# One-hots of node numbers on GpSimd instead of VectorE, and the merged rows' stores on ScalarE's queue, in the merge of a two-layer graph network

## The chip, the cores and the metric

One Trainium2 chip, one of its cores. The metric is the device time of one execution in microseconds; three runs of the kernel before are at hand. Engines are named as in the profile: PE is TensorE (PEld its weight loads), DVE is VectorE, ACT is ScalarE, POOL is GpSimd, SP is SyncE; a name with a q (SPq, ACTq, POOLq) is that engine's own instruction queue, where DMAs are issued.

## What is computed

The input is 50,000 nodes with 128 features, 50,000 edges sorted by target node, and 32 edge types. The change lies in the first layer, an attention layer with four heads:

```python
xl = (x @ Wl).reshape(n, H, C)
xr = (x @ Wr).reshape(n, H, C)
m = xl[src] + xr[dst]                       # edges, and a self loop for each node
e = leaky_relu(m, 0.2)
logits = einsum('ehc,hc->eh', e, att)
ex = exp(logits - amax[dst])
alpha = ex / (segment_sum(ex, dst) + 1e-16)
out = segment_sum(alpha * xl[src], dst)     # one row per node
# then a norm over all nodes (mean and variance of each feature), elu,
# layernorm of x + result, and a second graph layer with 2 rounds
```

## The kernel before, in words

The kernel is a sequence of stages; all five engines meet at the end of each (`end_stage`, `end_pool_stage`). Stage 0 projects all nodes (`xl_d`, `xr_d`), stage 1 works through the edges in 400 tiles and leaves in `w_d[0]` one row for each target node that has edges: 128 weighted sums, 4 denominators, 4 maxima, and the node's number in the last column (`WIDE` is 137). These rows are packed: the rows of a block of 128 nodes begin at a place that is looked up in `node_at`, and 128 rows from there hold all of that block.

Stage 2, the merge, is where the change lies. It puts the packed rows at their nodes, joins them with each node's self loop, and leaves `conv_d`. A tile is 128 nodes, a quad four tiles (98 quads, `QUADS`), a pair two quads (49 pairs, `PAIRS`), and a batch two pairs, so there are 24 full batches and one pair (`BATCHES` 25). For each pair:

- SP loads three of a quad's four tiles of packed rows (`load_sums`) and ACT's queue the fourth (`last_load`). The buffers hold six quads (`RING`), and a load for quad q waits until PE is done with quad q-6. SP also loads the nodes' own rows from `xl_d` (`load_own_rows`).
- DVE makes the one-hots (`pair_matrix`, lines 1872 to 1883): it subtracts the tile's first node number from the number column (L1877, once for each quad), and compares the result with 0 to 127 for all eight tiles in one instruction of 1024 columns (L1882). Two pairs of one-hots have room. It waits for the pair's packed rows and for PE to have used the one-hots of two pairs ago.
- PE multiplies one-hot by packed rows, one matmul for each tile (`gather_sums`, L1083), into two sets of PSUM banks by turns, and later adds up the merged rows and their squares over all nodes (`sums`, L1092).
- ACT copies PSUM into `agg_pair` and `dens` (`aggregated`, L1336 and L1337; it waits until the pair four back is merged), makes the exponentials of a batch (`share_exps`, L1343) and the squares of merged rows (`squares`, L1350).
- DVE computes the shares of edge sums and self loop for a batch (`share_args`, `share_values`, ten small instructions from L1891 to L1916), and merges a pair with three instructions of 1024 columns (`merged`, L1929, L1930, L1932), all of them on SBUF.
- POOL stores each merged quad to `conv_d` (L884), as soon as `cv_ok` says that its pair is merged. Semaphore `r["nh_out"]` counts the stores; `merged` waits for the stores of the pair three back, whose buffer it takes.

DVE's order is written out by hand: for batch v it is `pair_matrix(2v+2)`, `share_args(v)`, `share_values(v-1)`, `merged(2v-2)`, `pair_matrix(2v+3)`, `merged(2v-1)`. ACT's loop over pairs u is `aggregated` of both quads of pair u with a `last_load` behind each, then `squares` of the two quads of pair u-4, and every second time `share_exps`. `share_args(v)` needs `aggregated` of pair 2v+1, and that needs `merged(2v-3)`; so the two engines hand the work back and forth once in each batch. The stage ends with the norm's statistics on DVE and a square root on ACT (L1371), and stage 3 reads `conv_d` again.

Of the kernel before, what the change touches and what calls it, by code (L numbers as in the profile page):

```python
# [12 lines left out]
P = 128  # L13
# [39 lines left out]
def after(eng, sem, count):  # L53

    if not isinstance(count, int) or count > 0:
        eng.wait_ge(sem, count)
# [101 lines left out]
def gnn_kernel(nc, x, src, dst, etype, Wl, Wr, att, bias_conv, gn_weight, gn_bias, gn_mean_scale,  # L158
               basis, comp, loop_w, bias, out):
    ctx = ExitStack()  # L160
    with ctx:
# [240 lines left out]
        def pair_tiles(u):  # L402
            return quad_tiles(2 * u) + quad_tiles(2 * u + 1)
# [104 lines left out]
        def saved(l, q):  # L508

            return (q_in if q % RING // 3 else xl_out)[q % 3] if l else r["nh_out"][q % 3]  # L510

        def wait_saved(eng, l, q, stores):

            base = merged_counts["nh_out"][q % 3]
            eng.wait_ge(saved(l, q), (2 * base if l and q % RING < 3 else base) + 16 * stores)

        def wait_free(eng, l, q):

# [17 lines left out]
        def _(sp):  # L536
# [170 lines left out]
            sp.wait_ge(r["m_ps"], QUADS - 2)  # L707
            sp.wait_ge(cv_ok, PAIRS)
            for q in range(3):
                sp.wait_ge(r["nh_out"][q], 16)  # L710
                load_nx(q)
            end_stage(sp, 2)

# [58 lines left out]
        def _(pool):  # L772
# [104 lines left out]
            end_pool_stage(1)  # L877


            for q in range(QUADS):  # L880
                after(pool, r["nh_out"][q % 3], 16 * (q // 3))
                pool.wait_ge(cv_ok, q // 2 + 1)
                for to, part in node_quad(conv_d, q, of_pair(merged_pair, q), False):
                    pool.dma_start(to, part).then_inc(r["nh_out"][q % 3], 16)  # L884
            for k in range(3):
                pool.wait_ge(r["nh_out"][k], merged_counts["nh_out"][k])
            end_pool_stage(2)

            def inverse_row_deviation(q):
# [344 lines left out]
        def _(act):  # L1234
# [110 lines left out]
            def squares(q):  # L1345
# [3 lines left out]
                    act.wait_ge(cv_mm, q - 2)  # L1349
                act.activation(quad(4, q % 3)[:, 0:n, :], of_pair(merged_pair, q), ACT.Square).then_inc(cv_sq, 1)  # L1350

            def last_load(q):
                if q < QUADS:
                    if q >= RING:
                        act.wait_ge(r["m_ps"], q - RING + 1)
                    load_packed(act, -1, q, 3, 4)
            for q in range(4):
                last_load(q)
            for u in range(PAIRS + 4):
                if u < PAIRS:  # L1360
                    aggregated(2 * u)
                    last_load(2 * u + 4)
                    aggregated(2 * u + 1)
                    last_load(2 * u + 5)
                if u >= 4:
                    squares(2 * u - 8)
                    squares(2 * u - 7)
                if u % 2 and u < PAIRS or u == PAIRS - 1:
                    share_exps(u // 2)
            act.wait_ge(gn_var, 1)  # L1370
            act.activation(stat[:, 5, :], stat[:, 4, :], ACT.Sqrt).then_inc(gn_std, 1)  # L1371
            act.activation(join[:, 7, :], ones[0:1, 0:H], ACT.Exp)
# [151 lines left out]
        def _(dve):  # L1524
# [344 lines left out]

            dve.memset(work[12][:, 0:512], 0.0).then_inc(zeroed, 1)  # L1870

            def pair_matrix(u):
                n = pair_tiles(u)
                for q in (2 * u, 2 * u + 1):
                    at = slice(4 * q, 4 * q + quad_tiles(q))
                    wait_packed(dve, -1, q)
                    st.did(dve.tensor_tensor(node_rel[:, at], packed(q, WIDE)[:, 0:quad_tiles(q), WIDE - 1], node_base[:, at],  # L1877
                                             ALU.subtract))
                st.wait()
                if u >= 2:  # L1880
                    dve.wait_ge(r["m_ps"], 2 * u - 2)
                dve.tensor_tensor(sel_pair(u), lane[:, :].unsqueeze(1).to_broadcast([P, n, P]),  # L1882
                                  node_rel[:, 8 * u:8 * u + n].unsqueeze(2).to_broadcast([P, n, P]), ALU.is_equal).then_inc(pair_sel, 1)

            def share_args(v):

# [31 lines left out]
            def merged(u):  # L1918

                v, at = u // 2, slice(8 * (u % 2), 8 * (u % 2) + pair_tiles(u))  # L1920
                conv, xl = merged_pair(u), own_pair(u)
                edge, own = shares[:, v % 2, 0, at, :], shares[:, v % 2, 1, at, :]
                for q in (2 * u, 2 * u + 1):
                    wait_rows(dve, -1, q)
                    after(dve, r["nh_out"][q % 3], 16 * (q // 3 - 1))
                if u >= 3:
                    dve.wait_ge(cv_mm, 2 * u - 4)
                st.wait()
                st.did(dve.tensor_tensor(by_head(conv), by_head(agg_pair(u)), per_head(edge), ALU.mult))  # L1929
                st.did(dve.tensor_tensor(by_head(xl), by_head(xl), per_head(own), ALU.mult))  # L1930
                st.wait()
                dve.tensor_tensor(conv, conv, xl, ALU.add).then_inc(cv_ok, 1)  # L1932

            pair_matrix(0)
            pair_matrix(1)
            for v in range(BATCHES + 1):
                if 2 * v + 2 < PAIRS:
                    pair_matrix(2 * v + 2)
                if v < BATCHES:
                    share_args(v)  # L1940
                if v:
                    share_values(v - 1)
                    merged(2 * v - 2)
                if 2 * v + 3 < PAIRS:
                    pair_matrix(2 * v + 3)
                if v and 2 * v - 1 < PAIRS:
                    merged(2 * v - 1)

# [209 lines left out]
```

## Time and profile before

| | us |
|---|---|
| median of the three runs | 3206.0 |
| lowest, highest | 3199.38, 3206.53 |
| the profiled execution's own time | 3217.4 |
| its span from first to last instruction | 3215.5 |

| share of the span busy | PE | PEld | DVE | ACT | POOL |
|---|---|---|---|---|---|
| whole kernel | 89% | 64% | 79% | 51% | 53% |

```profile
## 2 busy tenths in 40 slices
PE   4898799999858888999799999699989999968897
PEld 4888688888735555888455555488845555536665
DVE  5999899999958897888677777544457777759998
ACT  2555223222224444999566666444446666645665
POOL 1110577777502222777777777322267777735554
PEclk9999899999979998999899999899999999989999
DMA  6999688888658886998333333399933333339997
```

Each slice is 80 us. The merge stands in slices 12 to 16 (from 904 us to 1262 us); in it the digits of PE and DVE are 8 and 9, DMA is at 8, ACT at 4 and POOL at 2. The profiled execution took 11 us more than the median; sums are made against its own time and then carried over to the median.

### The profile page before, as it was taken

How to read it: one execution, taken by the hardware profiler on the slowest of the kernel's cores; microseconds unless marked ns; L12 is line 12 of the kernel's file. 1: busy time of each engine (PE TensorE's matmuls, PEld its weight loads, DVE VectorE, ACT ScalarE, POOL GpSimd, SP SyncE). 2: the span in 40 equal slices, each digit the busy share in tenths (PEclk: the TensorE clock that was granted, in tenths of full speed). 3: DMA queues.
4: the chain of work that ended last, by engine and by line, in shares of the span. 5: the costliest groups of instructions: out<-in, count | busy, mean ns of one | idle time of the engine just before them, and what ended most of it. 6: DMA issues, size and time to landing. Idle time of an engine off the chain costs nothing.

```text
span 3215.5 us, 64715 instructions
## 1 busy us (share of the span) xinstructions
PE 2852.2 (89%) x16743; PEld 2059.8 (64%) x16743; DVE 2553.5 (79%) x7856; ACT 1654.8 (51%) x3920; POOL 1690.3 (53%) x2037
## 2 busy tenths in 40 slices
PE   4898799999858888999799999699989999968897
PEld 4888688888735555888455555488845555536665
DVE  5999899999958897888677777544457777759998
ACT  2555223222224444999566666444446666645665
POOL 1110577777502222777777777322267777735554
PEclk9999899999979998999899999899999999989999
DMA  6999688888658886998333333399933333339997
GB/s 170 263 278 274 160 186 184 186 182 184 155 150 237 244 243 202 293 293 273 97 104 104 104 103 104 91 298 304 298 105 104 104 103 104 104 84 328 331 341 259
DMA packets 744191, 621.24 MB, mean 193 GB/s; under 512 B 75517, under 2 KB 624622, under 8 KB 743822
## 3 DMA queue, kind: packets, MB, share of 16 engines
q1 hardware_dynamic: 546308, 361.80, 39.2%
q0 software_dynamic: 54208, 130.20, 15.0%
q10 hardware_dynamic: 143306, 125.07, 13.5%
q8 instruction: 140, 2.29, 0.3%
q14 instruction: 229, 1.88, 0.2%
HBM read 382.65 MB, written 234.13 MB: 192 GB/s over the span
## 4 chain that ended last, share of the span: by engine, by line
POOL 25%; DMA 21%; DVE 17%; issue 13%; PE 12%; ACT 8%; ACTq 2%; SPq 2%; DVEq 0%; POOLq 0%
POOL work L912 24%; DMA w_d<-work 15%; ACT work L1399 4%; PE bank L1202 3%; PE bank L1209 3%; DMA work<-w_d 3%; ACT work L1391 2%; DVE work L1784 2%; DVE work L1713 1%; DVE work L1715 1%; DVE self_logit L1717 1%; PE bank L1222 1%; DVE work L1929 1%; PE bank L1176 1%; DVE work L1930 1%
## 5 line engine op out<-in xcount | busy, mean ns | idle before, releaser
L2043 DVE SCALAR_TENSOR_TENSOR work<-bank,coef,work 128x128 f32<-128x128 f32 x2400 | 674.9, 344 | 242.3 <-ACT work L1433 239.0
L1155 PE MATMUL bank<-basis_s,work 128*128 128x512 f32 x1600 | 756.6, 596 | 1.8 <-ACT work L1426 1.8
L870 POOL DMA_INDIRECT work<-xl_d,slot_src x400 | 384.3, 961 | 204.1 <-issue 202.3
L912 POOL DMA_INDIRECT work<-x_d,slot_src x400 | 383.7, 959 | 126.3 <-issue 121.6
L912 POOL DMA_INDIRECT work<-h_d,slot_src x400 | 383.0, 957 | 123.8 <-issue 121.6
L1433 ACT ACTIVATE work<-bank,coef 128x128 f32<-128x128 f32 x800 | 294.0, 367 | 227.1 <-PE bank L1155 227.1
L1155 PEld LDWEIGHTS bank<-basis_s,work 128*128 128x128 f32 x1600 | 274.8, 192 | 197.2 <-issue 192.9
L1166 PEld LDWEIGHTS bank<-work 128*126 128x126 f32 x1600 | 207.6, 189 | 101.6 <-issue 100.9
L1209 PEld LDWEIGHTS bank<-work 128*128 128x128 f32 x1552 | 205.2, 193 | 97.1 <-issue 92.4
L884 POOL DMA_DIRECT2D conv_d<-work x99 | 73.8, 750 | 322.1 <-DVE work L1932 313.5
L1202 PE MATMUL bank<-work,loop_s 128*128 128x512 f32 x392 | 211.3, 621 | 33.9 <-ACT work L1473 33.1
L992 PE MATMUL bank<-work 96*128 96x125 f32 x1600 | 236.1, 276 | 0.0
L992 PEld LDWEIGHTS bank<-work 96*128 96x128 f32 x1600 | 217.4, 196 | 6.9 <-issue 0.2
L1146 PEld LDWEIGHTS bank<-ident,work 128*128 128x128 f32 x800 | 85.3, 142 | 206.4 <-DMA work<-x_d,slot_src 90.2
L1166 PE MATMUL bank<-work 128*126 128x128 f32 x1600 | 209.6, 274 | 5.5 <-ACT work L1439 3.2
L1473 ACT ACTIVATE work<-bank 128x512 f32<-128x512 f32 x196 | 114.8, 586 | 183.4 <-issue 133.5
L1209 PE MATMUL bank<-work 128*128 128x128 f32 x1552 | 206.3, 276 | 1.5 <-DMA work<-w_d 1.5
L1278 ACT ACTIVATE work<-bank 128x512 f32<-128x512 f32 x100 | 59.7, 597 | 256.7 <-issue 185.3
L929 POOL DMA_DIRECT2D h_d<-work x99 | 53.7, 543 | 247.0 <-DVE work L2077 243.1
L1092 PE MATMUL bank<-work,ones 128*128 128x512 f32 x392 | 179.2, 601 | 4.7 <-ACT work L1350 4.7
L1127 PE MATMUL bank<-work,ident 128*128 128x128 f32 (+1 forms) x782 | 162.3, 290 | 21.3 <-DVE work L1993 21.1
L2077 DVE COPY work<-bank 128x512 f32<-128x512 f32 x97 | 67.1, 692 | 135.7 <-PE bank L1222 135.7
(274 smaller groups left out, 6632.2 us busy)
## 6 DMA issues: line engine op xcount, KB each, us to landing
w_d<-work SPq DMA_DIRECT2D x800, 62.5 KB
work<-in_x_dram SPq DMA_DIRECT2D x194, 256.0 KB, 4.4
work<-x_d SPq DMA_DIRECT2D x194, 256.0 KB, 4.5
work<-xr_d ACTq DMA_DIRECT2D x388, 96.0 KB
w_d<-work SPq DMA_DIRECT2D x400, 66.9 KB
work<-w_d SPq DMA_DIRECT2D x398, 64.0 KB, 3.4
work<-w_d ACTq DMA_DIRECT2D x390, 64.0 KB, 3.4
xl_d<-work SPq DMA_DIRECT2D x97, 256.0 KB, 3.0
```

The source lines that it names most:

```text
L870: pool.indirect_dma_start(gathered(i)[:, c, :], None, xl_d, bass.IndirectOffsetOnAxis(ap=slot_src[:, a:a + 1], axis=0)).then_inc(e_in[i % ...
L912: pool.indirect_dma_start(quad(0, i % 3)[:, c, :], None, (x1_d, h1_d)[l], bass.IndirectOffsetOnAxis(ap=slot_src[:, a:a + 1], axis=0)).then ...
L992: last = pe.matmul(both[:, c * P + 1:c * P + 1 + TE], window(c, i)[:, h, :], turned_pick(h, i)[:, c, :], start=False, stop=h == 1, skip_gr ...
L1092: last = pe.matmul(psum[b][:, 0:whole * D], ones[:, :], rows[:, 0:whole, :].rearrange("p t d -> p (t d)"), start=False, stop=False, skip_g ...
L1127: pe.matmul(to[0:rows, at], ident[0:rows, 0:rows], skip_rows(q)[0:rows, t, :], start=True, stop=False)
L1155: pe.matmul(psum[YBANKS[k % 5]][:, :], quad(1, i % 2)[:, c, :], basis_s[:, l, :, :].rearrange("k b n -> k (b n)"), start=True, stop=True). ...
L1166: last = pe.matmul(psum[5 + c // per_bank][0:SLOTS, o:o + width], quad(4, i % 3, SLOTS)[:, c, :], quad(2, i % 3, width)[:, c, :], start=Tr ...
L1202: pe.matmul(to[:, 0:m], loop_s[:, l, :], work[7][:, (q % 2) * 512:(q % 2) * 512 + m], start=True, stop=False, skip_group_check=True)
L1209: last = pe.matmul(at, packed(q, D)[:, t, :], sel.rearrange("r (t p) -> r t p", t=4), start=False, stop=t == n - 1, skip_group_check=True)
L1399: last = act.activation(quad(8, k)[0:rows, t, :], psum[2 + q % 4][0:rows, t * D:(t + 1) * D], ACT.Identity, bias=norm[0:rows, k, 1, t:t + ...
L1433: act.activation(quad(2, i % 3, width)[:, c, 0:D], psum[YBANKS[k % 5]][:, 0:D], ACT.Copy, scale=coef[:, i, l, c, 0:1]).then_inc(r["first"], 1)
L2043: ins = dve.scalar_tensor_tensor(o, psum[YBANKS[k % 5]][:, b * D:(b + 1) * D], coef[:, i, l, c, b:b + 1], o, ALU.mult, ALU.add)
```

## The change

All one-hots of the stage are made by POOL instead of DVE: the same two subtractions for a pair, then one comparison for each tile (`tensor_scalar` with the tile's column as its scalar, 128 columns each) in place of one comparison of 1024 columns. POOL no longer stores merged rows. ACT stores a quad right after its squares, on its own DMA queue; the stores are counted on `xr_out`, which stage 0 has used and left at `merged_counts["nh_out"]`. ACT waits for all stores before the square root. The waits of DVE (`merged`) and of SP (first loads of stage 3) are moved to the new semaphore, and `wait_saved` of the later layers counts `nh_out` from zero.

```diff
@@ sync
             for q in range(3):
-                sp.wait_ge(r["nh_out"][q], 16)
+                sp.wait_ge(xr_out[q], merged_counts["nh_out"][q] + 16)
                 load_nx(q)
@@ gpsimd
-            for q in range(QUADS):
-                after(pool, r["nh_out"][q % 3], 16 * (q // 3))
-                pool.wait_ge(cv_ok, q // 2 + 1)
-                for to, part in node_quad(conv_d, q, of_pair(merged_pair, q), False):
-                    pool.dma_start(to, part).then_inc(r["nh_out"][q % 3], 16)
-            for k in range(3):
-                pool.wait_ge(r["nh_out"][k], merged_counts["nh_out"][k])
+            def pair_matrix(u):
+                n = pair_tiles(u)
+                for q in (2 * u, 2 * u + 1):
+                    at = slice(4 * q, 4 * q + quad_tiles(q))
+                    wait_packed(pool, -1, q)
+                    st.did(pool.tensor_tensor(node_rel[:, at], packed(q, WIDE)[:, 0:quad_tiles(q), WIDE - 1], node_base[:, at],
+                                             ALU.subtract))
+                st.wait()
+                if u >= 2:
+                    pool.wait_ge(r["m_ps"], 2 * u - 2)
+                for t in range(n):
+                    last = pool.tensor_scalar(sel_pair(u)[:, t, :], lane[:, :], node_rel[:, 8 * u + t:8 * u + t + 1], None, ALU.is_equal)
+                last.then_inc(pair_sel, 1)
+            for u in range(PAIRS):
+                pair_matrix(u)
             end_pool_stage(2)
@@ scalar
+            def save_merged(q):
+                act.wait_ge(xr_out[q % 3], merged_counts["nh_out"][q % 3] + 16 * (q // 3))
+                for to, part in node_quad(conv_d, q, of_pair(merged_pair, q), False):
+                    act.dma_start(to, part).then_inc(xr_out[q % 3], 16)
+
@@
                 if u >= 4:
                     squares(2 * u - 8)
+                    save_merged(2 * u - 8)
                     squares(2 * u - 7)
+                    save_merged(2 * u - 7)
                 if u % 2 and u < PAIRS or u == PAIRS - 1:
                     share_exps(u // 2)
+            for k in range(3):
+                act.wait_ge(xr_out[k], 2 * merged_counts["nh_out"][k])
             act.wait_ge(gn_var, 1)
@@ vector
                     wait_rows(dve, -1, q)
-                    after(dve, r["nh_out"][q % 3], 16 * (q // 3 - 1))
+                    if q >= 6:
+                        dve.wait_ge(xr_out[q % 3], merged_counts["nh_out"][q % 3] + 16 * (q // 3 - 1))
@@
-            pair_matrix(0)
-            pair_matrix(1)
             for v in range(BATCHES + 1):
-                if 2 * v + 2 < PAIRS:
-                    pair_matrix(2 * v + 2)
                 if v < BATCHES:
                     share_args(v)
                 if v:
                     share_values(v - 1)
                     merged(2 * v - 2)
-                if 2 * v + 3 < PAIRS:
-                    pair_matrix(2 * v + 3)
                 if v and 2 * v - 1 < PAIRS:
                     merged(2 * v - 1)
```

## Rows read from the trace of the kernel before

**Rows 1.** Stretch view: busy us and (instructions) of PE, PEld, DVE, ACT, POOL, clock, DMA, GB/s.

```profile
940.00:1222.00 282.00, 240.31 (x1002) 146.59 (x1000) 252.63 (x461) 119.89 (x435) 61.50 (x83) 0.96 0.84 241
```

**Rows 2.** Chain of work: start us, us, what; first and last steady L1929.

```profile
932.98 1.23 DVE work L1929
...
1230.55 1.23 DVE work L1929
```

**Rows 3.** Timeline of DVE, one batch: start us, us, instruction.

```profile
1161.97 0.20 DVE L1891 TENSOR_SCALAR merge_s<-dens 128x64 f32<-128x64 f32 x1
...
1164.59 1.23 DVE L1929 TENSOR_TENSOR work<-work,shares 128x1024 f32<-128x1024 f32 x1
1165.73 1.22 DVE L1930 TENSOR_TENSOR work<-work,shares 128x1024 f32<-128x1024 f32 x1
1166.99 1.22 DVE L1932 TENSOR_TENSOR work<-work 128x1024 f32<-128x1024 f32 x1
...
1168.39 1.22 DVE L1882 TENSOR_TENSOR work<-lane,node_rel 128x1024 f32<-128x1024 f32 x1
```

**Rows 4.** View of waits from 940 to 1222 us: in total, times, longest.

```profile
ACT work L1336 <- DVE work L1932: 136.8, 42, 4.9
...
DVE node_rel L1877 <- DMA work<-w_d: 17.0, 17, 2.7
```

**Rows 5.** Timeline of ACT, same batch.

```profile
1159.85 0.39 ACT L1336 ACTIVATE work<-bank 128x256 f32<-128x256 f32 x1 [1.80 <-DVE work L1932]
...
1168.31 0.38 ACT L1336 ACTIVATE work<-bank 128x256 f32<-128x256 f32 x1 [4.83 <-DVE work L1932]
...
1170.30 1.15 ACT L1350 ACTIVATE work<-work 128x512 f32<-128x512 f32 x2 [0.18 <-issue]
```

**Rows 6.** Line view: ACT's stores of 256 KB in stage 3 (min/median/max ns).

```profile
L1406 ACTq DMA_DIRECT2D x_d<-work x99: 326/326/452, 1276.8 to 1536.1; - x99
```

**Rows 7.** DMA queues from 940 to 1222 us: packets, MB, share of 16 engines.

```profile
q1 hardware_dynamic: 81133, 39.96, 53.6%
q0 software_dynamic: 6650, 21.76, 21.7%
```

**Rows 8.** DMA queues from 60 to 250 us, stage 0.

```profile
q1 hardware_dynamic: 101398, 50.35, 96.0%
```

**Rows 9.** Line views of POOL instructions: count, min/median/max ns, starts, shapes.

```profile
L834 POOL TENSOR_SCALAR work<-work,type_of x25: 1531/1535/1961, 35.0 to 263.2; 128x500 f32<-128x500 bf16 x25
...
L777 POOL TENSOR_SCALAR_AFFINE_SELECT ident<-ident x1: 287/287/287, 1.5 to 1.5; 128x128 f32<-128x128 f32 x1
...
L925 POOL TENSOR_TENSOR norm<-norm x98: 192/199/201, 2901.5 to 3205.6; 128x4 f32<-128x4 f32 x97, 128x3 f32<-128x3 f32 x1
```

**Rows 10.** Timeline of POOL and DVE in stage 0: both held up.

```profile
68.76 0.69 DVE L1784 TENSOR_TENSOR work<-work 128x512 f32<-128x512 f32 x1
...
68.98 1.87 POOL L834 TENSOR_SCALAR work<-work,type_of 128x500 f32<-128x500 bf16 x1 [30.94 <-PE bank L1036]
...
69.49 1.05 DVE L1713 SCALAR_TENSOR_TENSOR work<-work 128x512 f32<-128x512 f32 x1
```

**Rows 11.** The same at 168 us: neither held up.

```profile
168.31 1.53 POOL L834 TENSOR_SCALAR work<-work,type_of 128x500 f32<-128x500 bf16 x1 [7.05 <-PE bank L1036]
...
168.93 0.69 DVE L1784 TENSOR_TENSOR work<-work 128x512 f32<-128x512 f32 x1
```

**Rows 12.** Timeline of DVE and POOL in stage 3.

```profile
1326.93 0.69 DVE L1993 SCALAR_TENSOR_TENSOR work<-work 128x512 f32<-128x512 f32 x1
1327.11 0.60 POOL L894 TENSOR_SCALAR norm<-moments 128x4 f32<-128x4 f32 x1 [0.86 <-DVE norm_arg L2012]
```

**Rows 13.** Line view of L884, the stores of merged rows on POOL's queue.

```profile
DMA to landing us min/median/max: 2.8/4.2/6.6
```

**Rows 14.** Timeline at the stage's end: last squares, last variance step.

```profile
1251.60 1.04 ACT L1350 ACTIVATE work<-work 128x512 f32<-128x512 f32 x2 [3.21 <-DVE work L1932]
...
1259.44 0.29 DVE L1969 SCALAR_TENSOR_TENSOR stat<-stat 128x128 f32<-128x128 f32 x1
```

More of the change, by code:

```diff
@@ L514, in wait_saved @@
             base = merged_counts["nh_out"][q % 3]
-            eng.wait_ge(saved(l, q), (2 * base if l and q % RING < 3 else base) + 16 * stores)
+            eng.wait_ge(saved(l, q), (0 if not l else 2 * base if q % RING < 3 else base) + 16 * stores)
         def wait_free(eng, l, q):
@@ L1870, in _ @@
             dve.memset(work[12][:, 0:512], 0.0).then_inc(zeroed, 1)
[L1872 to L1883, printed above, removed]
             def share_args(v):
```

## The prediction

> **What bounds the kernel now.** I read the page first, to place the stage: the change touches only the merge, some 358 us of a span of 3215.5. Then the stretch view over the stage's steady part, 940 to 1222 us [rows 1]: DVE is busy 252.6 of 282 us (90%), PE 240.3 (85%), the DMA engines 84%, ACT 119.9 (43%), POOL 61.5 (22%). Three resources are near full. That is what a reader is to keep in mind: who takes load off the fullest meets the next two at once.
>
> The chain of waits gives the beat. L1929 of the first pair starts at 932.98 and that of pair 44 at 1230.55 [rows 2]; between them lie 22 batches, so 297.6 / 22 = **13.5 us for a batch**. The timeline of one batch [rows 3, 5] shows how it is made up. The shares start at 1161.97, `merged` at 1164.59, its last instruction ends at 1166.99 + 1.22 = 1168.21; so shares cost 2.62 us and `merged` 3.62. Then come one-hots (L1882 at 1168.39), the second `merged`, and one-hots again. ACT starts a pair's `aggregated` 0.1 us after `merged` ends (1168.31), is through it at 1170.30 (2.0 us, a load issue behind each quad included) and has made the squares at 1171.45. For the odd pair it starts at 1159.85, and DVE's shares follow at 1161.97, 2.1 us later. In the view of waits ACT stands 136.8 us for `merged` [rows 4]; DVE stands only 17.0 us, and for late packed rows. So DVE is the bound, and the beat is DVE's sum.
>
> **What is taken away.** DVE loses per batch two comparisons of 1.22 us and four subtractions, about 3.0 us with their gaps, and the wait for packed rows, 17.0 us over 21 batches, 0.8 a batch. What is next to be late? Without one-hots `merged` follows `merged`. From the end of the first one (call it M), DVE ends the second at M + 3.6. ACT meanwhile does `aggregated` 2.1 and squares 1.15, free at M + 3.3, so it starts the odd pair's `aggregated` at M + 3.7 and the shares start at M + 5.8. Add 2.6 and 3.6: the round closes after **12.0 us**. That is the new beat if nothing else is slower: 1.5 us less, 33 us over 22 batches. It is not to be had in full: PE's work for a batch is 240.3 / 282 x 13.5 = 11.5 us and the DMA engines' 0.84 x 13.5 = 11.3.
>
> **The stores.** On POOL's queue the stores moved 21.76 MB in 21.7% of 282 us, 2.8 us a MB, in packets of 3.3 KB; rows of 512 bytes on SP's queue take 96.0% of 190 us for 50.35 MB, 3.6 us a MB [rows 7, 8]. A batch stores 1.05 MB, so on ACT's queue the DMA engines need about 0.85 us more, 12.15 in all. With three resources between 11.5 and 12.15 in a round of 12.0 I take 12.6 as the best beat that can be had. The issue costs ACT little: 0.33 us each [rows 6], issued while the square before it (0.6 us) still runs; bounds are 0 and four times 0.33. ACT's new wait is for the store three quads back, issued over a pair earlier, so it has landed; behind that wait stand the next squares, `share_exps` and `aggregated`, and for them PE and DVE. Packed rows that ACT loads now queue behind two stores of 256 KB; they are needed a batch later. `merged` waits for stores of the pair three back, now issued by ACT two iterations before it is needed: covered. I put the stores at nothing while the beat is above 13.
>
> **What is added: POOL's work.** For a batch it is 16 comparisons of 128 columns and four subtractions. The nearest row is L834, the same instruction (`is_equal` against a column scalar), 500 columns in 1.53 us [rows 9]. Scaled with the columns alone it gives 0.39 us for 128; the row's own split, below, gives 0.13 + 1.40 x 128/500 = **0.49 us**. Ends: 0.29 us (L777, 128x128 in and out, another operation) and 0.56 (if the 0.2 us of L925 is a fixed part and the rest scales). I take 0.49, by the same operation; its input is bf16 where the new one is f32, which is why the lower end stays open. A subtraction is 0.2 us (L925), four with their semaphore waits 1.0. POOL's free time for a batch: 16 x 0.49 + 1.0 = 8.8 us, well under 13.5 by itself. It would be hidden if POOL and DVE did not meet.
>
> They do meet, and the trace shows it. L834 starts at 68.98 beside L1784, which has two inputs in SBUF and ends at 69.45 [rows 10]. L834 then takes 1.87 us instead of 1.53; its end lies 1.40 us behind L1784's end, and in the ten cases of this kind (of 25) the distance is 1.40 or 1.41. L894 (four columns) ends at 1327.71, 0.09 behind the end of L1993, and takes 0.60 us for what is otherwise 0.2 [rows 12]. So **POOL waits until a DVE instruction with two SBUF inputs has ended.** The other way round: L1713, started 0.04 us after L1784, takes 1.05 instead of 0.69, so DVE is held 0.36 us by L834 (five cases, 0.32 to 0.37). But L1784 that starts 0.62 us into L834 is not held at all [rows 11]. So POOL holds DVE for the first part only, until about 0.13 + 0.42 us of 1.53; 0.42 us is 500 columns, so for 128 I take **0.11 us**.
>
> All three instructions of `merged` have two SBUF inputs. Beside 1.22 us of such work POOL gets one comparison: it waits for the end, takes 0.11 us while the next DVE instruction is held, computes on, and its next one waits again. In two `merged` POOL thus makes six comparisons, and they take 6 x (1.22 + 0.11) = 8.0 us. The other ten, 4.9 us, and the 1.0 us of subtractions must lie where DVE doesn't hold it: beside the shares (small instructions, I add 0.4 us for blocks) and while DVE waits for ACT. Sum: 8.0 + 4.9 + 1.0 + 0.4 = **14.3 us for a batch, POOL being the bound.** Late one-hots stop PE, then ACT, then the shares, so the time that POOL lacks appears as idle time of DVE.
>
> The Trainium skill, "SBUF — State Buffer", section "SBUF: two separate sides", speaks against this change: a DVE instruction with two SBUF inputs and a GpSimd instruction that reads SBUF exclude each other, and whoever starts first has the shared port pair for its whole instruction. The trace agrees on POOL's waiting, but not on DVE's: it was held 0.36 us by an instruction that went on for 1.4 [rows 10].
>
> **Start and end of the stage.** The first pair's one-hots, which nothing hides, take DVE 1.22 us as all do; POOL needs 8 x 0.49 = 3.9, 2.7 more. The next three pairs come with their loads and should hide most of theirs. I add 4 us; bounds 1 and 4 x 2.7 = 11. At the end ACT waits for the last stores before the square root: last squares end at 1252.6, the variance is there at 1259.7 [rows 14], and a store takes 4.2 us to land, 6.6 at most [rows 13], so this costs 0; at most 1, should the square root's table load come behind the wait.
>
> **The sum.** (14.3 - 13.5) x 22 = +17, +4 for the start: +21 us. The profiled execution's 3217.4 would become 3238; against the median of 3206.0, 11 lower, **3227**.
>
> **The rivals.**
> 1. *The gain comes through.* If a comparison costs 0.3 us and its hold on DVE falls into gaps, the beat is 12.6: -0.9 x 22 = -20, +4 at the start, 3190. For: POOL's 0.29 us row; the holds are short. Against: with POOL in the middle of DVE's back-to-back work each hold is DVE's loss. Deciding point: beat below 13.1. Chance 0.22.
> 2. *Break-even.* A comparison costs under 0.38 us, so POOL keeps up, but its holds lie in DVE's round: 12.0 + 6 x 0.11 + some 0.4 beside the shares = 13.1. -0.4 x 22 + 4 = -5, 3201. Chance 0.20.
> 3. *The forecast*, POOL the bound at 14.3, 3227, its own range 3216 to 3238. Chance 0.35.
> 4. *POOL doesn't get between back-to-back instructions.* L1930 starts 0.09 us before L1929 ends [rows 3], with no wait between; if POOL gets in only behind L1930 and L1932, it makes four in two `merged` and twelve outside: 7.8 + 5.9 + 1.4 = 15.1, +35 + 4, 3245. Chance 0.15.
> 5. *Each holds the other for its whole instruction.* Then 7.3 us of `merged`, POOL's 8.8 and at most the shares' 2.6 stand one behind another: 18.7, +114 + 4, 3324. Against it: DVE was held for 0.36 us only, and once not at all [rows 10, 11]. Chance 0.08. It is the rule of the Trainium skill that is named above, taken in full.
>
> That the change doesn't do what it says I leave out: the one-hots and stores are the same, only their engines differ.
>
> **How the numbers follow.** The likeliest is 3227. Low end 3186 (rival 1 with a beat of 12.4: -24 + 4), high end 3263 (rival 4 at 0.56 us a comparison: 15.9, +53, with the start's 4). About 0.3% (10 us) is what a measurement can tell: faster 0.22, same 0.20, slower 0.58.
>
> **What would show it.** In the profile after: the distance of L1929 from batch to batch (14.3; 12.6; 13.1; 15.1; 18.7); POOL's comparison at its shortest (0.49) and its median, which should be well above it, with ends just behind ends of `merged`; durations of L1929 to L1932 at 1.33 instead of 1.22; PE's `gather_sums` waiting for POOL; `aggregated` waiting for PE, not for DVE. Rival 1 is right if PE and DMA are above 90% and POOL idles. I am wrong in the first step if a comparison of 128 f32 columns costs 0.3 us, and in the second if the DVE instructions are not longer than before. Stores are wrongly priced if ACT's idle time is ended by them.

## The result and the profile after

| | before | after |
|---|---|---|
| median of the runs, us | 3206.3 | 3288.9 |
| lowest, highest | 3199.38, 3208.07 | 3285.72, 3290.73 |
| the profiled execution's own time | 3217.4 | 3285.7 |
| its span | 3215.5 | 3283.9 |

The ratio is 1.0263 [1.0247, 1.0278]: slower by 82.6 us. The direction was forecast, the size was not: 3227 was the value, 3263 the upper end.

In the code after, POOL's subtraction is L885 and its comparison L891; `gather_sums` is L1091 (before L1083) and `sums` L1100, `aggregated` L1344 and L1345, `squares` L1358, the stores L1363 on ACT's queue, the first share instruction L1896, and `merged` L1935, L1936 and L1938 (before L1929, L1930, L1932). First the page: totals and slices of 82 us.

```profile
PE 2882.1 (88%) x16743; PEld 2092.6 (64%) x16743; DVE 2492.7 (76%) x7709; ACT 1656.3 (50%) x3920; POOL 1973.1 (60%) x2427
...
PE   4998799999667777899799999889989999978887
...
DVE  5999899999645556788677777734457777758998
...
POOL 1110677777388997477777777512257777744554
...
DMA  7999577777466776799533333379943333329997
```

The merge fills slices 12 to 16. POOL is at 7 to 9 there, where it was at 0 and then at 2. Behind slice 12, in which the stage began, PE was at 8, DVE at 7 to 9 and DMA mostly at 8; now PE is at 7, DVE at 5 and 6, and DMA at 6 and 7. The stretch view of the steady part gives the numbers (columns as in [rows 1]):

```profile
940.00:1280.00 340.00, 251.54 (x974) 166.68 (x975) 195.61 (x320) 118.69 (x424) 305.16 (x407) 0.90 0.70 191
```

POOL is busy 305 of 340 us (90%), DVE 58%, PE 74%, DMA 70%. Three resources were near their limit; now one is, and it is a new one. The view of waits from 940 to 1260 us says what stands behind what (in total, times, longest):

```profile
DVE merge_s L1896 <- ACT dens L1345: 127.6, 19, 7.5
ACT work L1344 <- PE bank L1091: 102.4, 38, 5.4
PEld bank L1091 <- POOL work L891: 101.3, 19, 6.6
...
POOL node_rel L885 <- DMA work<-w_d: 29.3, 19, 2.5
```

Read from the third line up: PE waits for POOL's one-hots, ACT for PE's sums, DVE for ACT's copies. DVE's wait of 6.7 us a batch is time that POOL lacks. The beat, from the timeline of DVE, L1935 of the first pair and of pair 44 (start us, us):

```profile
931.08 1.22 DVE L1935 TENSOR_TENSOR work<-work,shares 128x1024 f32<-128x1024 f32 x1
...
1302.16 1.23 DVE L1935 TENSOR_TENSOR work<-work,shares 128x1024 f32<-128x1024 f32 x1
```

371.1 / 22 = **16.87 us for a batch** instead of 13.53 [rows 2]: +73.5 us. That is the loss. From the stage's first subtraction to the first `merged` it is 31.3 us instead of 25.4 (+5.9), and from pair 44 to PE's first matmul of the norm 33.1 instead of 31.6 (+1.5). Stage 1 ended 7.8 us earlier in this execution (the first subtraction starts at 899.77 instead of 907.59), and the stages behind took 4.7 less, both with code that the change doesn't touch: 73.5 + 5.9 + 1.5 - 7.8 - 4.7 = 68.4, the difference of the two spans. The rest, up to 82.6, is that the profiled execution before was 11 us above its median and the one after 3 below.

What POOL does in a batch is in its timeline (instructions of one line in a row are put together, x8):

```profile
1100.50 0.20 POOL L885 TENSOR_TENSOR node_rel<-work,node_base 128x4 f32<-128x4 f32 x1 [1.30 <-DMA work<-w_d]
1100.80 9.96 POOL L891 TENSOR_SCALAR work<-lane,node_rel 128x128 f32<-128x128 f32 x8
...
1111.16 4.64 POOL L891 TENSOR_SCALAR work<-lane,node_rel 128x128 f32<-128x128 f32 x8
...
1117.26 0.20 POOL L885 TENSOR_TENSOR node_rel<-work,node_base 128x4 f32<-128x4 f32 x1 [1.27 <-DMA work<-w_d]
```

From 1100.80 to the next batch's comparisons at 1117.55 there are 16.75 us: eight comparisons beside the two `merged`, 9.96; subtractions, 0.4; eight comparisons clear of `merged`, 4.64; subtractions and a wait for packed rows, 1.75. The two sets of eight are the same work, and one takes more than twice as long. Taken one by one (timeline of POOL):

```profile
1100.80 0.72 POOL L891 TENSOR_SCALAR work<-lane,node_rel 128x128 f32<-128x128 f32 x1
1101.50 2.51 POOL L891 TENSOR_SCALAR work<-lane,node_rel 128x128 f32<-128x128 f32 x1
1103.99 2.41 POOL L891 TENSOR_SCALAR work<-lane,node_rel 128x128 f32<-128x128 f32 x1
1106.39 1.33 POOL L891 TENSOR_SCALAR work<-lane,node_rel 128x128 f32<-128x128 f32 x1
1107.70 1.33 POOL L891 TENSOR_SCALAR work<-lane,node_rel 128x128 f32<-128x128 f32 x1
```

And DVE at the same time:

```profile
1101.27 1.23 DVE L1935 TENSOR_TENSOR work<-work,shares 128x1024 f32<-128x1024 f32 x1
1102.41 1.22 DVE L1936 TENSOR_TENSOR work<-work,shares 128x1024 f32<-128x1024 f32 x1
1103.66 1.23 DVE L1938 TENSOR_TENSOR work<-work 128x1024 f32<-128x1024 f32 x1
1104.80 1.22 DVE L1935 TENSOR_TENSOR work<-work,shares 128x1024 f32<-128x1024 f32 x1
1105.94 1.31 DVE L1936 TENSOR_TENSOR work<-work,shares 128x1024 f32<-128x1024 f32 x1
1107.28 1.27 DVE L1938 TENSOR_TENSOR work<-work 128x1024 f32<-128x1024 f32 x1
```

The comparison that starts at 1101.50 ends at 1104.01, 0.38 us behind the end of L1936 (1103.63); it has let the end of L1935 (1102.50) pass, where L1936 had already started at 1102.41. The next one lets the end of the first L1938 pass, and gets in behind L1935 (1106.02). The two after it get in at 1107.25 and 1108.55. So in the 7.3 us of two `merged` POOL gets in at four of six ends. Over the whole stage it is the same: in 20 of the 22 batches two comparisons take over 2 us and two some 1.33, in the other two it is one and three.

### The profile page after: what moved, and what is told of

The parts are those of the page before. It is cut to its first block, busy times and chain, and to the rows that moved or that the text cites. A ratio compares the mean times of both kernels' runs of the same rounds, so it can differ in the third digit from the quotient of the medians.

```text
span 3283.9 us, 64963 instructions
## 1 busy us (share of the span) xinstructions
PE 2882.1 (88%) x16743; PEld 2092.6 (64%) x16743; DVE 2492.7 (76%) x7709; ACT 1656.3 (50%) x3920; POOL 1973.1 (60%) x2427
## 4 chain that ended last, share of the span: by engine, by line
POOL 44%; issue 16%; DVE 13%; PE 13%; ACT 7%; DMA 4%; ACTq 2%; SPq 1%; DVEq 0%; POOLq 0%
POOL work L920 23%; POOL work L870 11%; POOL work L891 10%; ACT work L1416 4%; PE bank L1210 3%; PE bank L1217 3%; DVE work L1801 2%; DVE work L1730 2%; DVE work L1732 2%; DVE self_logit L1734 2%; ACT work L1408 1%; PE bank L1230 1%; PE bank L1184 1%; DVE work L2095 1%; DMA w_d<-work 1%
## 5 line engine op out<-in xcount | busy, mean ns | idle before, releaser
L891 POOL TENSOR_SCALAR work<-lane,node_rel 128x128 f32<-128x128 f32 x391 | 338.7, 885 | 4.8
L1217 PEld LDWEIGHTS bank<-work 128*128 128x128 f32 x1552 | 207.0, 194 | 97.7 <-issue 93.0
L1091 PE MATMUL bank<-work 128*128 128x136 f32 x782 | 141.3, 352 | 115.0 <-POOL work L891 115.0
L1091 PEld LDWEIGHTS bank<-work 128*128 128x128 f32 x782 | 133.8, 254 | 145.7 <-POOL work L891 135.2
L1344 ACT ACTIVATE work<-bank 128x256 f32<-128x256 f32 x196 | 72.0, 388 | 257.6 <-PE bank L1091 145.2
```

Source lines behind the costliest of these rows:

```text
L891: last = pool.tensor_scalar(sel_pair(u)[:, t, :], lane[:, :], node_rel[:, 8 * u + t:8 * u + t + 1], None, ALU.is_equal)
L1091: last = pe.matmul(psum[2 + 2 * (q % 2) + t // 2][:, o:o + D + 2 * H], of_pair(sel_pair, q)[:, t, :], packed(q, WIDE)[:, t, 0:D + 2 * H], ...
L1217: last = pe.matmul(at, packed(q, D)[:, t, :], sel.rearrange("r (t p) -> r t p", t=4), start=False, stop=t == n - 1, skip_group_check=True)
```

## The experiments

The theory: POOL is the bound, since it waits for DVE's instructions with two SBUF inputs, and late packed rows come on top. Against it stand that the stores on ACT's queue do it; that the wait for packed rows only fills time which POOL has anyway; that comparisons are slow beside DVE for another reason than the kind of its operands; and that it is the fixed cost of so many small instructions. In the expectations A is the theory, and other letters are what an experiment sets against it. "Batch" is always the mean over the same 22; each ratio is to the kernel before on the same chip.

**1. The stores alone** (the kernel before with `save_merged` on ACT; DVE keeps the one-hots).

```diff
-            for q in range(QUADS):
-                after(pool, r["nh_out"][q % 3], 16 * (q // 3))
...
                     squares(2 * u - 8)
+                    save_merged(2 * u - 8)
                     squares(2 * u - 7)
+                    save_merged(2 * u - 7)
```

> One part of the change alone: DVE keeps the one-hots, only the stores move from POOL's queue to ACT's. Theory A (the whole loss is POOL's one-hots, with POOL waiting for VectorE's two-input instructions): the stores cost nothing, 3206 within 6 us, batches stay at 13.5 us. Rival B (part of the loss is the stores: packets of 512 bytes need more DMA time and ACT waits for their landing): 3216 to 3230, packed rows arrive later and DVE's wait for them grows from 17 us to 30 or more.

Measured: 3209.8 against 3215.0, ratio 0.9986 [0.9975, 0.9996]; batch 13.29. The stretch from 940 to 1222 us:

```profile
940.00:1222.00 282.00, 241.38 (x1020) 151.42 (x1020) 257.38 (x466) 122.93 (x448) 0.00 (x0) 0.96 0.90 245
```

The DMA engines go from 84% [rows 1] to 90%, 0.6 us a batch, and nobody waits for them longer: the wait for packed rows [rows 4] is not among the large ones any more. With the stores moved, DVE stands for packed rows 0.5 us in all where it was 17.0; why they come earlier with the DMA engines busier is open. So the stores by themselves cost nothing in the batch. They do have a part at the stage's end. ACT's table load for the square root stands behind the variance here too, where it lay behind the last squares before:

```profile
1254.32 1.28 ACT L1373 ACT_TABLE_LOAD   x1 [7.18 <-DVE stat L1972]
```

That is some 1.3 us. The rest of the loss needs the one-hots on POOL. The one-hots alone, with the stores left on POOL's queue, were not run, so what the two do only together is not told apart.

**2. The wait for packed rows** (the kernel after; ACT's queue loads its tile two quads earlier).

```diff
-            for q in range(4):
+            for q in range(RING):
                 last_load(q)
...
-                    last_load(2 * u + 4)
+                    last_load(2 * u + 6)
                     aggregated(2 * u + 1)
-                    last_load(2 * u + 5)
+                    last_load(2 * u + 7)
```

> The changed kernel, with ACT's fourth-tile loads issued one pair earlier (they are for pair u+3 in ACT's iteration u instead of u+2). In the changed kernel a batch takes 16.9 us, and in it POOL waits some 1.4 us for packed rows. Theory A says that POOL is the bound, so each us that it doesn't wait comes off the batch: 15.5 to 15.7 us, total 3256 to 3265. Rival C (POOL's wait is only a gap that a later wait would fill, for PE or ACT): less than 8 us gained, 3281 or more.

Measured: 3258.8 against 3215.0, ratio 1.0138 [1.0117, 1.0160]; batch 15.30. The stretch, and the line view of its subtraction:

```profile
940.00:1222.00 282.00, 216.24 (x883) 137.87 (x884) 180.24 (x291) 108.35 (x388) 278.36 (x370) 0.93 0.79 212
...
L885 POOL TENSOR_TENSOR node_rel<-work,node_base 128x4 f32<-128x4 f32 x74 | 13.1, 200 | 0.0
```

POOL is busy 278 of 282 us and waits for no packed rows. The wait was worth 1.6 us a batch, nearly half of the loss of 3.3, and it is of a new kind. In the kernel after, ACT issues the load for pair u+2 behind `aggregated` of pair u, that waits for `gather_sums`, and that for POOL's one-hots; so POOL waits for a load that its own lateness has made late. The transfer itself is not slower: such a load lands 2.3 us after its issue in the median, where it was 3.4 before the change. The eight comparisons beside `merged` still take 9.7 to 10.1 us.

The kernel after shows one more link in that chain, TensorE's clock (timelines of PE and of ACT's queue, and a stretch of that time):

```profile
1101.11 2.02 PE L1091 MATMUL bank<-work 128*128 128x136 f32 x16
...
1110.81 3.31 PE L1091 MATMUL bank<-work 128*128 128x136 f32 x16 [4.25 <-POOL work L891]
...
1114.61 0.40 ACTq L467 DMA_DIRECT2D work<-w_d  x1
...
1112.50:1114.20 1.70, 1.70 (x9) 1.70 (x8) 0.00 (x0) 0.70 (x5) 1.70 (x4) 0.50 0.17 41
```

The columns of the last line are those of [rows 1]; the last but two is the granted clock. Behind PE's wait for one-hots (4.25 us) it is at 0.50, and `gather_sums` takes 3.31 us for a pair, where ten microseconds before it took 2.02 at 1.00. ACT's copy and the load stand behind it, and POOL then waits 1.27 us for that load. Of POOL's 21 waits for packed rows between 930 and 1300 us, 20 come behind a `gather_sums` of 3.1 to 3.9 us. As an estimate from these rows, most of the 1.5 us a batch that POOL waits is the 1.0 to 1.9 us that the lower clock adds there; no run takes it away by itself.

**3. The port** (the kernel after; the shares go to PSUM, so that two of `merged`'s three instructions read one input from PSUM and only the last, L1941 here, has two in SBUF).

```diff
+            share_ps = psum[6][:, 0:256].rearrange("p (v k t h) -> p v k t h", v=2, k=2, t=16)
...
-                edge, own = shares[:, v % 2, 0, at, :], shares[:, v % 2, 1, at, :]
+                edge, own = share_ps[:, v % 2, 0, at, :], share_ps[:, v % 2, 1, at, :]
```

> The changed kernel, with the shares written to a free PSUM bank, so that L1935 and L1936 read one operand from SBUF and one from PSUM and only L1938 still has two SBUF inputs. DVE's work stays the same size. Theory A (POOL stands behind two-input instructions of DVE): the eight comparisons that take 9.9 us beside the merge shrink to 6 to 7.5, a batch to 13.3 to 14.5 us, total 3210 to 3237. Rival D (POOL is slow by itself and through its late packed rows, and its waiting for DVE matters little): batch 16 us or more, total 3270 or more.

Measured: 3217.4 against 3215.0, ratio 1.0011 [0.9999, 1.0023]; batch 13.28. Nothing of POOL's work is taken away, DVE's instructions are the same in number and size, and 3.6 us of 16.87 are gone. (With the 1.6 of experiment 2 this is more than the loss: the two overlap, since POOL is no longer the only bound here, and `gather_sums` mostly takes 2.13 us again.) POOL's timeline:

```profile
1095.92 4.69 POOL L891 TENSOR_SCALAR work<-lane,node_rel 128x128 f32<-128x128 f32 x8
...
1101.01 5.53 POOL L891 TENSOR_SCALAR work<-lane,node_rel 128x128 f32<-128x128 f32 x8
...
1102.74 1.48 POOL L891 TENSOR_SCALAR work<-lane,node_rel 128x128 f32<-128x128 f32 x1
```

DVE's:

```profile
1102.53 1.23 DVE L1941 TENSOR_TENSOR work<-work 128x1024 f32<-128x1024 f32 x1
1103.67 1.22 DVE L1938 TENSOR_TENSOR work<-work,bank 128x1024 f32<-128x1024 f32 x1
```

The eight comparisons beside `merged` take 5.4 to 6.4 us instead of 10. The only long one in this stretch starts 0.2 us into L1941 and ends 0.46 behind its end (1103.76), though the next `merged` has begun: an instruction with one input in PSUM (`bank`) doesn't shut POOL out.

**4. Only the early loads, in the kernel before.** The same edit as in 2.

> The kernel before, with ACT's fourth-tile loads one pair earlier, as in the run above. DVE waits there 17 us for packed rows between 940 and 1222 us. If the cause of that wait is the place of ACT's loads behind its copies, it goes and the total is 3206 - 15 = 3191; if it is the DMA engines' load (84% busy), nothing moves: 3203 to 3209.

Measured: 3208.5 against 3215.0, ratio 0.9978 [0.9966, 0.9990]; batch 13.16. DVE's wait for packed rows (0.8 us a batch [rows 4]) is gone, but it brings only 0.37 a batch, less than I expected; in exchange DVE waits 12.4 us of 282 for ACT's `dens`, where it was 2.0.

**5. Edits 2 and 3 together, in the kernel after.**

> The changed kernel with both cures at once: shares in PSUM (batch 13.3 us alone) and ACT's loads a pair earlier (15.3 us alone, from 16.9). With both, POOL's work in a batch is 2 x 4.64 us of comparisons, some 0.9 of subtractions and at most 2 us of waiting for L1938: 12.2 us, below what PE (11.5) and the DMA engines (12.2) allow by little. Theory A: batch 12.5 to 12.9 us, 8 to 15 us faster than the kernel before on the same chip (ratio 0.995 to 0.9975). Rival E (DMA load and the round trip between DVE and ACT hold it where the run with PSUM alone stands): 13.2 us, ratio 0.999 to 1.001.

Measured: 3196.5 against 3201.6, ratio 0.9979 [0.9967, 0.9990]; batch 12.96. A gain, but of 5 us, where I expected 8 to 15. Stretch and waits:

```profile
940.00:1222.00 282.00, 246.97 (x1038) 150.79 (x1036) 209.79 (x351) 126.28 (x457) 244.04 (x423) 0.97 0.89 245
...
POOL node_rel L885 <- DMA work<-w_d: 23.6, 16, 3.2
```

The median batch takes 12.7 us; two of 14.5 and 16.9 lift the mean. With DMA at 89%, PE at 88% and POOL at 87% that median is close to the prediction's best beat, 12.6.

**6. Half of the pairs on each engine** (the kernel after with early loads, shares in SBUF; DVE makes the even pairs' one-hots, POOL the odd pairs').

```diff
-                last.then_inc(pair_sel, 1)
-            for u in range(PAIRS):
+                last.then_inc(pool_sel, 1)
+            for u in range(1, PAIRS, 2):
                 pair_matrix(u)
...
-                pe.wait_ge(pair_sel, q // 2 + 1)
+                pe.wait_ge(pool_sel if q // 2 % 2 else pair_sel, q // 4 + 1)
```

> One-hots split: DVE makes those of the even pairs, in the gap in which it waits for ACT, and POOL those of the odd pairs; ACT's loads a pair earlier; shares stay in SBUF. POOL has 8 comparisons a batch, so it cannot be the bound, and the batch should fall to DVE's round of 12.0 us plus a few holds, that is to the 12.6 us that PE and the DMA engines allow: ratio to the kernel before 0.993 to 0.996. If POOL's comparisons, each standing behind the merge (9.9 us for eight) and then started late, still stop PE, the batch is 13.2 us or more and the ratio 0.998 or more.

Measured: 3222.3 against 3201.6, ratio 1.0054 [1.0036, 1.0073]; batch 14.23. A miss: I expected a gain. The median batch takes 13.0 us; seven of the 22 take 15.7 to 18.9 and make the loss. POOL has half the comparisons, but eight of them still take up to 11.0 us where they fall beside `merged`, 13 of the 21 sets 8.4 or more; one of them:

```profile
1094.42 9.80 POOL L892 TENSOR_SCALAR work<-lane,node_rel 128x128 f32<-128x128 f32 x8
```

POOL also waits for packed rows here, 88.5 us of 282. So halving its load doesn't help enough: one pair's one-hots start late and then take long once they meet `merged`, and PE waits for them (52.5 us of 282). Which of the two counts is seen in 7.

**7. The same with the shares in PSUM.** Edit 3 added to 6.

> The split of the run above, with the shares in PSUM too. If the port is what remains to be lost in that run, this one is faster by 0.2 to 0.4 us a batch (5 to 9 us in all); if PE and the DMA engines are the bound by then, the two are the same within 3 us.

Measured: 3197.1 against 3201.6, ratio 0.9985 [0.9971, 0.9998]; batch 13.14. From 6 to 7 it is 25 us, where I expected less than 10 from the port: with half the work on POOL the port still made the loss. POOL's wait for packed rows is even longer in 7, 140.9 us of 282, so that wait by itself is not what cost the time in 6.

**8. What a comparison costs by its size** (the kernel after, each comparison over 64 columns).

```diff
-                    last = pool.tensor_scalar(sel_pair(u)[:, t, :], lane[:, :], node_rel[:, 8 * u + t:8 * u + t + 1], None, ALU.is_equal)
+                    last = pool.tensor_scalar(sel_pair(u)[:, t, 0:64], lane[:, 0:64], node_rel[:, 8 * u + t:8 * u + t + 1], None, ALU.is_equal)
```

> The changed kernel, with each comparison made over the first 64 of its 128 columns only; the other half of the one-hots is left out, so the sums of those nodes are not made. It tells what a comparison consists of. If half of its 0.58 us is fixed (a line through 500 columns in 1.53 us and 128 in 0.58 gives 0.25 us fixed and 2.6 ns a column), it takes 0.42 us, and a pair clear of the merge 3.3 us instead of 4.64. Theory A: beside the merge the waits rule, not the width: eight comparisons there still take 7.5 to 9.5 us, a batch 14.5 to 15.7 us, total 3238 to 3262. Rival F (the width is what counts there too): both stretches halve, batch 13.5 us or less, total 3217 or less.

Measured: 3255.0 against 3201.6, ratio 1.0156 [1.0132, 1.0181]; batch 15.96. Line view (min/median/max ns) and two stretches of the timeline:

```profile
L891 POOL TENSOR_SCALAR work<-lane,node_rel x391: 430/440/2568, 900.4 to 1272.6; 128x64 f32<-128x64 f32 x196
...
1099.77 7.75 POOL L891 TENSOR_SCALAR work<-lane,node_rel 128x64 f32<-128x64 f32 x8
...
1107.93 3.31 POOL L891 TENSOR_SCALAR work<-lane,node_rel 128x64 f32<-128x64 f32 x8
```

In a row it is 3.31 / 8 = 0.41 us for 64 columns and 4.64 / 8 = 0.58 for 128, so about 0.25 us fixed and 2.6 ns for a column. Half the columns take 0.9 us off a batch, far from half of POOL's 15: the waits stay. Seven of the twenty sets of eight beside `merged` take 7.75 us like the one shown, the others 8.9 to 9.2, against 9.7 to 10.1 for nearly all at 128 columns. The comparisons that wait through two instructions take 2.34 to 2.54 us, at 128 columns 2.38 to 2.73. (The batch is a little above the 14.5 to 15.7 that I expected, because POOL now waits 2.8 us a batch for packed rows, 49.6 in 282, where it was 1.5.)

**9. A gap at every end** (the kernel after; DVE waits on a semaphore ahead of each of the three instructions, so that none starts before the one ahead has ended).

```diff
                 st.wait()
+                if u:
+                    dve.wait_ge(cv_ok, u)
                 st.did(dve.tensor_tensor(by_head(conv), by_head(agg_pair(u)), per_head(edge), ALU.mult))
+                st.wait()
                 st.did(dve.tensor_tensor(by_head(xl), by_head(xl), per_head(own), ALU.mult))
```

> The changed kernel, with a semaphore wait of DVE on its own instruction before each of the three instructions of a merge (before, only L1938 had one). DVE gets about 0.1 us more to do at four places of a batch. Theory A2 (POOL can step in where DVE's next two-input instruction has not been started yet, and mostly not between instructions that overlap): POOL gets in at each of the six ends, the eight comparisons beside the merge take 8.0 to 8.7 us instead of 9.9, a batch 15.6 to 16.3 us instead of 16.9, total 3262 to 3280, and the three instructions grow to 1.3 us each. Rival G (a waiting POOL gets in or not regardless of gaps): the stretch stays at 9.7 or more, and the total at 3286 or more.

Measured: 3277.9 against 3209.9, ratio 1.0220 [1.0200, 1.0240]; batch 16.22. POOL's comparisons, one by one:

```profile
1102.80 1.56 POOL L891 TENSOR_SCALAR work<-lane,node_rel 128x128 f32<-128x128 f32 x1
1104.34 1.33 POOL L891 TENSOR_SCALAR work<-lane,node_rel 128x128 f32<-128x128 f32 x1
```

In the batch shown all six that meet `merged` take 1.33 to 1.56 us. Of all comparisons between 940 and 1260 us none takes over 1.7 us, where in the kernel after 36 take over 2: with a gap at the end POOL gets in at each. Yet the eight take mostly 9.1 to 9.5 us (8.6 to 9.7 in all) instead of 9.96, because the gaps lengthen the two `merged` from 7.3 to 7.8 us; I had expected 8.0 to 8.7. So the two missed ends cost about 0.65 us a batch, and the rest of the port's price is there with every end used.

**10 to 12. In search of a faster one.** 10 is the kernel before with the stores on ACT and the early loads; 11 is number 5, and 12 is number 7, with SP loading the nodes' own rows two quads later, so that packed rows come first:

```diff
-            for q in range(QUADS + 8):
+            for q in range(QUADS + 10):
...
-                if q >= 8:
-                    load_own_rows(q - 8)
+                if q >= 10:
+                    load_own_rows(q - 10)
```

> The kernel before with stores on ACT's queue and ACT's loads a pair earlier, DVE keeping the one-hots. Each of the two alone gave a batch of 13.3 and 13.15 us. DVE's own work is 13.1 us, so together they give no more than 13.1: ratio 0.997 to 0.998, as the early loads alone. If the stores' change had a gain of its own (POOL's descriptors off the DMA engines), it would be 0.996 or less.

> The fastest kernel so far (all one-hots on POOL, shares in PSUM, early loads; batch 12.96 us in the mean, most 12.5, some 14.5 and 16.9), with SP's loads of own rows issued two quads later. SP stands up to 6 us before such a load until a merge has freed its buffer, and loads of packed rows queue behind. If that makes the long batches, they go and the mean falls to 12.5 to 12.6 us: ratio 0.994 to 0.996. If the long batches come from the DMA engines' load (89% busy), nothing moves: 0.997 to 0.999.

> The same change of SP's order in the kernel with split one-hots, shares in PSUM and early loads (batch 13.1 us in the mean, most 12.5, some 15 to 17.7). With the long batches gone 12.4 to 12.5 us, ratio 0.993 to 0.995; otherwise 0.998.

Measured, each against 3209.9: 3207.4, ratio 0.9988 [0.9977, 1.0000], batch 13.30; 3209.9, 0.9998 [0.9989, 1.0008], batch 13.15; 3207.9, 0.9993 [0.9983, 1.0003], batch 13.33. The gains of 1 and 4 don't add: each of the two already takes away the same wait of DVE for packed rows. In 11 and 12 the longest batches are gone (at most 14.2 in 11, two of 14.6 and 15.2 in 12), but the others are longer (medians 13.2 and 13.4 instead of 12.7 and 12.6), and `merged` now waits for own rows, 13.6 us of 282 in 11 and 18.2 in 12. Both are misses: I had expected the mean to fall. The fastest are 5 and 4, at 0.9979 and 0.9978, not to be told from each other, nor surely from 7 and 1 (0.9985, 0.9986); 4 changes three lines.

## Why the prediction was right about the sign and wrong about the size

**Right.** POOL became the bound, by waiting for the two-input instructions; PE waits for POOL, ACT for PE, DVE for ACT, as the marks said. The stores cost nothing in the batch (1). The holds on DVE are small: L1935, L1936 and L1938 mean 1.24, 1.26 and 1.25 us between 940 and 1260 us, against 1.22 [rows 3], not the 1.33 that I had named as a sign. A round without one-hots on DVE is near the 12.6 that I named once POOL keeps up (5, median 12.7).

**Wrong: POOL's sum for a batch, 14.3 where it is 16.9.** Step by step:
- *The comparison, 0.49 us.* In a row it is 0.58, above even the upper end of 0.56. I had taken the split of L834 [rows 9] as 0.13 fixed and the rest by columns; 8 shows 0.25 fixed. For the eight clear comparisons this is 4.64 against 3.92, +0.7.
- *Six comparisons beside two `merged`, 8.0 us.* With two more to make the pair full, 9.0 by the prediction, and 9.96 is measured: +1.0. Of the mechanism's two halves, 1.22 + 0.11 = 1.33 for a comparison that waits is what the trace shows to the hundredth, but only where POOL gets in at each end, and to the hundredth by luck: the holds in that batch are 0.05 and 0.09 us, not 0.11, and a gap of 0.03 comes on top. It gets in at four of six, and two take 2.4 us. Four is the count of rival 4, to which I gave 0.15; I had its evidence in L1930 starting before L1929 ends [rows 3], and left it out of the forecast. The ends are not quite the rival's: POOL misses two of the three ends at which the next instruction has already started, not all three. Experiment 9 shows the cause by putting the gaps in.
- *The wait for packed rows, counted as saved.* I booked DVE's 0.8 us a batch as a gain and never asked who waits for the rows next. POOL does, and longer, since ACT's load now hangs on POOL itself: 1.5 us a batch by the view of waits (29.3 us in 320), 1.6 by experiment 2. TensorE's lower clock behind each wait for one-hots lengthens it (2); that was in no term either.
- *Subtractions and blocks, 1.4 us.* About 0.9 without the wait: -0.5.

Together 14.3 + 0.7 + 1.0 + 1.5 - 0.5 = 17.0, against 16.87. The largest part is the one that was no part of the sum at all. Rival 4 (15.1, at its upper end 15.9) doesn't reach the result either: it leaves the wait out, and its comparison is too cheap too.

**The start** cost 5.9 us for 4, in its bounds: 0.7 of that is the dearer comparison. **The end** cost 1.5 us, where I had 0 and at most 1. The case named for it came: the square root's table load now stands behind the waits.

```profile
1331.60 1.28 ACT L1388 ACT_TABLE_LOAD   x1 [7.18 <-DVE stat L1969]
```

It starts behind the variance, where before it ran at 1252.7, right behind the last squares. The one-hots have no part in it: with the stores alone on ACT the load stands there too (1), and with the early loads alone (4) it does not. I had bounded it by 1 us, though the load takes 1.28.

**The rule of the Trainium skill** ("SBUF — State Buffer", "SBUF: two separate sides") was nearer than I gave it credit for on POOL's side: experiment 3 removes 3.6 us a batch by one PSUM operand. It has the two exclude each other for a whole instruction, and on DVE's side the runs disagree with that: the comparison that waits for L1936's end (1107.25) goes on until 1107.72, and L1938, started at 1107.28, takes 1.27 us instead of 1.22. Taken in full it gave 3324, and the time is 3289.

**What stays open.** Why the mean of 5, 7, 11 and 12 stays at 13.0 to 13.3, where the median of 5 and 7 is 12.6 or 12.7: batches wait for loads with the DMA engines near 0.9, and with one kind of load put ahead another comes late; which transfer holds which up was not settled. And why POOL gets in behind L1935 in the second `merged` and not in the first.

## What to carry to other kernels

Before work goes to GpSimd, look at what VectorE does beside it: next to back-to-back instructions with two SBUF inputs a GpSimd comparison cost the time of one or two of VectorE's, with 64 columns as with 128, and one operand in PSUM for two of VectorE's three instructions gave that back (16.87 to 13.28 us a batch). Where a wait of the relieved engine is booked as saved, follow the awaited thing to its new consumer, and see whether its producer now hangs on that consumer, with TensorE's clock after a wait as part of that path. An engine that moves 16 small instructions in place of 2 large ones pays a fixed part sixteen times: read it from a row of the same shape, or bound it from above more widely.

## What the hardware showed that I had not expected

- GpSimd can wait through two of VectorE's instructions: 2.41 and 2.51 us for a comparison of 0.58, where VectorE's next two-input instruction starts about 0.1 us before the last one ends; at one of the three such ends in the batch shown it still gets in.
- A comparison on GpSimd costs 0.25 us and 2.6 ns for a column of f32 (64 and 128 columns).
- `merged` with the shares read from PSUM is not slower on VectorE: 1216 and 1212 ns in experiment 3, against 1.22 us with both inputs in SBUF.
- TensorE's granted clock in the merge fell from 0.96 [rows 1] to 0.90 of 2.4 GHz. PE was busy 5.8 us of the 10 from 1101.16 on, the rest waiting for one-hots; in the 4.64 us behind that, the clock was 0.63, a mean between the two levels (0.5 is 1.2 GHz), and `gather_sums` took 3.31 us instead of 2.02. That lay on the path: the load that POOL waited for was issued behind it.
